# Row gathers regrouped into bursts of 8, 12 and 12, and a part of the second layer moved, in a DLRM interaction tower

## What is computed

```python
e = stack([tbl_f[ids[:, f]] for f in range(27)], axis=1)      # 2048 x 27 x 128
dot = einsum('bnd,bmd->bnm', e, e)                             # 2048 x 27 x 27
z = the 351 entries of dot with n < m
h = concatenate([z, dense_ctx], axis=1)                        # 2048 x 367
h = maximum(h @ W_top1 + b_top1, 0)                            # 367 x 512
h = maximum(h @ W_top2 + b_top2, 0)                            # 512 x 256
y = h @ W_top3                                                 # 256 x 1
```

## Time and profile before

| | us |
|---|---|
| median of 3 executions | 512.14 (509.94 to 519.04) |
| profiled execution, own time | 503.7 |
| its span | 501.9 |
| mean granted TensorE clock | 0.864 of full speed |

### The profile page before, as it was taken

How to read it: one execution, slowest core, us unless ns; L and a number is a source line. 1 busy time by engine, 2 the same in 40 slices (tenths; PEclk the granted TensorE clock), 3 DMA queues, 4 the chain that set the end, 5 groups by cost and what they waited for, 6 DMA issues and landing times.

```text
span 501.9 us, 14882 instructions
## 1 busy us (share of the span) xinstructions
PE 377.5 (75%) x6214; PEld 340.0 (68%) x6214; DVE 234.1 (47%) x505; ACT 130.5 (26%) x165; POOL 286.9 (57%) x264
## 2 busy tenths in 40 slices
PE   2578466289569977699919995699786988299997
PEld 2477356189458966499707984689675987289786
DVE  4766081257215663166612872165631636338241
ACT  2265010124012232033301340122320313123432
POOL 5888667763455744465663845467544767638300
PEclk9959579579788997799957997799967999789999
DMA  7995312212112131133122131132211231111100
GB/s 193 271 253 147 120 46 74 53 34 96 34 44 76 47 106 31 31 86 110 32 52 63 44 106 37 37 76 56 96 36 28 74 120 32 49 26 35 28 1 0
DMA packets 22270, 36.18 MB, mean 72 GB/s; under 512 B 12662, under 2 KB 13310, under 8 KB 22252
## 3 DMA queue, kind: packets, MB, share of 16 engines
q1 hardware_dynamic: 13996, 19.01, 13.2%
q0 software_dynamic: 8256, 16.92, 12.8%
HBM read 35.90 MB, written 0.01 MB: 72 GB/s over the span
## 4 chain that ended last, share of the span: by engine, by line
PE 66%; issue 21%; another core or an unknown queue 4%; DMA 3%; DVE 2%; ACT 2%; SPq 1%; ACTq 0%; DVEq 0%
PE emb_ps L693 30%; PE gram_ps L738 13%; PE mlp_ps L761 7%; PE emb_ps L729 5%; PE mlp_ps L775 3%; PE emb_ps L709 3%; DMA ids_b<-in_ids_mm 3%; PE mlp_ps L783 2%; DVE onehot L564 2%; PE emb_ps L828 1%; PE mlp_ps L745 1%; ACT embT L459 1%; SPq L276 1%; PE emb_ps L840 1%
## 5 line engine op out<-in xcount | busy, mean ns | idle before, releaser
L415 POOL DMA_INDIRECT rows<-in_tbl,idx x256 | 279.9, 1093 | 181.4 <-PE gram_ps L738 53.3
L693 PE MATMUL emb_ps<-onehot,parts 125*128 125x256 f32 x1280 | 171.8, 294 | 34.5 <-issue 15.1
L693 PEld LDWEIGHTS emb_ps<-onehot,parts 125*128 125x128 f32 x1280 | 163.7, 198 | 42.9 <-issue 22.3
L564 DVE TENSOR_SCALAR onehot<-ids_b,row_of 128x512 fp32r<-128x512 int32 x320 | 131.1, 483 | 85.7 <-PE emb_ps L693 46.8
L738 PE MATMUL gram_ps<-embT 128*32 128x26 f32 x4096 | 72.3, 217 | 79.0 <-issue 78.9
L738 PEld LDWEIGHTS gram_ps<-embT 128*32 128x32 f32 x4096 | 61.4, 136 | 93.3 <-issue 93.1
L451 ACT ACTIVATE embT<-emb_ps 128x512 f32<-128x512 f32 x40 | 49.0, 1224 | 141.4 <-PE emb_ps L693 91.6
L586 DVE STREAM_TRANSPOSE turned<-gram_ps 128x832 f32<-128x832 f32 x16 | 16.8, 1050 | 128.9 <-PE gram_ps L738 121.1
L459 ACT ACTIVATE embT<-emb_ps 128x512 f32<-128x512 f32 x32 | 36.8, 1241 | 81.2 <-PE emb_ps L729 62.8
L580 DVE COPY embT<-emb_ps 128x512 f32<-128x512 f32 x32 | 36.1, 1184 | 22.0 <-PE emb_ps L729 9.7
L729 PE MATMUL emb_ps<-ident,rows 128*128 128x128 f32 x256 | 36.2, 296 | 4.2 <-issue 3.1
(11 more groups left out here) (40 smaller groups left out, 105.7 us busy)
## 6 DMA issues: line engine op xcount, KB each, us to landing
ids_b<-in_ids_mm SPq DMA_DIRECT2D x8, 896.0 KB
ids_b<-in_ids_mm SPq DMA_DIRECT2D x16, 256.0 KB
rows<-in_tbl,idx POOLq DMA_INDIRECT x256
embT<-in_tbl SPq DMA_DIRECT2D x6, 448.0 KB
w_sb<-in_tbl SPq DMA_DIRECT2D x2, 448.0 KB
turned<-in_tbl SPq DMA_DIRECT2D x1, 560.0 KB
w_sb<-in_W_top SPq DMA_DIRECT2D x1, 512.0 KB
turned<-in_tbl SPq DMA_DIRECT2D x1, 448.0 KB
```

The lines of the kernel that those rows point to most:

```text
L415: pool.indirect_dma_start(rows[:, t, n, :], None, tables[f], bass.IndirectOffsetOnAxis(idx[:, t, f:f + 1], 0), engine_sem=gathers_written) ...
L564: last = nc.vector.tensor_scalar(onehot[:, k % OH:k % OH + LOOK_TABLES, c, :], ids_b[:, k:k + LOOK_TABLES, :], row_of[:, c:c + 1], None, A ...
L693: last = nc.tensor.matmul(emb_ps[BANK[k]][:, m * W:(m + 1) * W], parts[0:MP, f, part, c * D:(c + 1) * D], onehot[0:MP, f % OH, c, :], star ...
```

## The change

POOL's waits are regrouped. Counted again from the pair before, no gather follows the transposes of tile 0; eight (groups 0 and 1 of tile 0) follow Gram 0, twelve (groups 2 and 3 of tile 0, group 0 of tile 1) follow Gram 1, and twelve (groups 1 to 3 of tile 1) follow lookup 4 of the pair itself. A wait of POOL at the end of pair 0 goes, which the first group of pair 1 now has itself. On TensorE four of the eight calls of the second layer go ahead of the transposes of tile 1.

```diff
-CALLS_AFTER = [{3: 6}, {3: 8}]
+CALLS_AT = [{NT: 6}, {0: 4, NT: 4}]
...
                 if isinstance(p, int) and p == 0:
                     return
-                if t == 0:
-                    if k == 1:
-                        pool.wait_ge(emb_filled, (p - 1) * JOBS + row_job(0, NT - 1) + 1)
-                    elif k == 2:
-                        pool.wait_ge(gram_filled, (p - 1) * TILES + 1)
-                    elif k == 3:
-                        pool.wait_ge(emb_filled, (p - 1) * JOBS + row_job(1, NT - 1) + 1)
-                elif k == 0:
-                    pool.wait_ge(gram_filled, p * TILES)
+                if t == 0 and k % 2 == 0:
+                    pool.wait_ge(gram_filled, (p - 1) * TILES + 1 + k // 2)
+                elif t and k == 1:
+                    pool.wait_ge(emb_filled, p * JOBS + 4)
                 else:
-
-                    pool.wait_ge(emb_filled, p * JOBS + k)
+                    return
                 pool.sem_inc(pool_waited, 1)
...
-                if first:
-
-                    pool.wait_ge(gram_filled, 1)
-                    pool.sem_inc(pool_waited, 1)
...
                 for t in range(TILES):
                     calls = 0
-                    for k in range(NT):
-                        transpose_rows(p, t, k)
-                        for _ in range(0 if first else CALLS_AFTER[t].get(k, 0)):
+                    for k in range(NT + 1):
+                        for _ in range(0 if first else CALLS_AT[t].get(k, 0)):
                             (first_layer_rest, second_layer)[t](p - 1, calls)
                             calls += 1
+                        if k < NT:
+                            transpose_rows(p, t, k)
                     gram(p, t)
```

## The result

| | before | after |
|---|---|---|
| median of 4 executions, us | 511.04 (506.94 to 519.04) | 568.07 (563.42 to 571.22) |
| profiled execution, own time / span, us | 503.7 / 501.9 | 571.22 / 569.4 |
| mean granted TensorE clock | 0.864 | 0.823 |

The ratio is 1.114, 95% interval 1.102 to 1.126: slower by 57 us. The forecast was 506.0 us in a range of 489 to 531, so it was wrong, and the nearest of the rivals is the first (near 560). The profiled execution of before is one of its fastest (503.7 against a median of 511.04), so the two spans differ by more than the medians, 67.5 us.

A forecast was written before the change was run, and what follows sets the result against it. TensorE held 66% of the chain of waits, and a Gram under gathers was taken to stall until they end. Pair 1 -7.0, five steady pairs -5.0, pair 7 +5.9: -6.1, so 506 us, range 489 to 531.

The forecast's parts named there:

- The burst of twelve behind Gram 1: Twelve gathers under lookups 1 to 3; lookups bear it, nothing taken, range 0 to 2 us a pair.
- The window of 16.4 us: Twelve gathers from 158.9 to 175.3 in the kernel before, with TensorE busy throughout; taken as showing that lookups bear gathers.
- The first rival: Burst behind Gram 1 stalls the lookups as in pair 1: about 9.5 us in six pairs, near 560; chance 0.22.
- The pause of 2 us: Behind Gram 1, between four gathers and twelve more in the kernel before; its loss was priced at nothing.
- The rest of the steady pair: Gram 0 ends at 42.7 instead of 43.4, Gram 1 gains nothing; 1.0 us less a pair, -5.0 for five.
- Its trickle ending 1.2 us behind a gather: Gram 0 of pairs 2 to 6 stays in two pieces, its slow part ending 1.2 us behind the last gather.
- The half second layer: Four calls ahead of tile 1's transposes, 1 to 2 us, hidden by Gram 1's trickle; worth nothing.
- Pair 1: Shorter gather run, TensorE back near 95.9 instead of 102.1: 6.2 us, with Gram 0's 0.7 us taken as -7.0.
- the second burst's part: Twelve gathers behind lookup 4: Gram 0 meets their tail and ends 0.7 us earlier, also counted in pair 1.
- Pair 7: Gram 0, free of gathers before, now meets the burst behind lookup 4 and ends at 484.3 instead of 478.4: +5.9 us.
- Second rival: One-hots block a gather, Gram 0 slips through early: 2.1 to 3.5 us less in six pairs, 490 to 498; chance 0.20.
- Third rival: Pair 1's stall doesn't form: pair 1 takes 58 instead of 76 us, -18 instead of -7, 495 total; chance 0.13.

The follow-up runs named there:

- e15: Changed kernel with a 128 x 256 scratch fill on POOL ahead of only the twelve gathers behind Gram 1: 509.24 us, ratio 1.012.
- e10: Changed kernel with POOL filling a 128 x 256 scratch tile ahead of each gather: 489.94 us, ratio 0.962.
- e14: Changed kernel with a small 128 x 8 scratch fill on POOL ahead of each gather: 573.75 us, ratio 1.136.
- e17: Changed kernel with a 128 x 128 scratch fill on POOL ahead of each gather: 556.70 us, ratio 1.089.
- e1: Changed kernel with the burst of twelve behind Gram 1 paused after four gathers, until lookup 1 is done: 512.13 us, ratio 1.015.
- e4: Changed kernel with eleven extra one-hot operations a pair on VectorE, written to a tile nobody reads: 523.31 us, ratio 1.038.
- e5: Changed kernel with the burst behind Gram 1 paused after eight gathers, until lookup 2 is done: 547.51 us, ratio 1.066.
- e3: Kernel before with only the second layer's four calls moved ahead of tile 1's transposes: 508.27 us, ratio 1.011.
- e16: Changed kernel with the 128 x 256 fill ahead of each gather and without the wait for lookup 4: 482.81 us, ratio 0.946.
- e2: Kernel before without POOL's three waits for lookups 1 to 3, so sixteen gathers follow Gram 1 in one run: 597.62 us, ratio 1.185.

## Why the prediction was wrong

**The step that failed** is "The burst of twelve behind Gram 1 ... By the 16.4 us window the lookups bear it; I take nothing, with 0 to 2 us a pair as the range". It costs 10 us a pair in pairs 2 to 6: lookup 3 ends at +24.1 in place of +14.1, and with this burst alone spaced (e15) the loss goes from 11.4 to 1.2%. The window of 16.4 us was right and was read for the wrong thing. There VectorE made one-hots, so its gathers lay 1.41 us apart on average ((174.39 - 158.93) / 11); behind Gram 1 VectorE is idle and they lie 1.25 apart. I had both figures in the same paragraph (16.4 us "under one-hots", "at the pitch without them" 15.0 us) and used them for the burst's length only, not as a difference in kind. Which of the two spacings is safe is what e10, e14 and e17 show.

**The first rival** named the pattern, the place and the price: 9.5 us a pair against 10.4 measured. On top of the forecast that gave 555 us in the profiled execution and 563 in the median, against 571.2 and 568.1. What it lacked is mostly in pair 7, where its stall met the later Gram 0. It got 0.22. What I held against it, that the burst begins behind a finished Gram and not under one, was not evidence: no row of before showed a long run of close gathers under lookups that was harmless. The only such run, in pair 1, had stalled. With that said the rival should have been the forecast.

**The pause of 2 us** stood in the prediction ("There stood four, a pause of 2 us, and twelve more"), and I priced its loss at nothing. e1 shows that it is worth ten per cent of the time. As e1, e4 and e5 read together, it lets lookup 1's signal out, VectorE starts, and from then on VectorE's work keeps the gathers apart. That order of causes is my reading; a pause that waits for no signal wasn't tried, and in pairs 1 and 7 of the changed kernel the signal came in time and lookup 3 was late even so. e5 shows that its place matters.

**The rest of the steady pair**, judged by e1, where lookups are whole: predicted 57.4 on average, measured 59.3 (57.4 to 62.9). Gram 0 was to end at +42.7 and ends at +42.6 in pair 2, which is luck, by two errors that cancel: the burst ended at +36.8 instead of +38.8, since its gathers lay 1.31 us apart and not 1.41, and Gram 0 came 5.8 us behind it instead of 3.9, in one piece and not in two. "Its trickle ending 1.2 us behind a gather" is wrong there: the signals of tile 0's transposes are late under a close burst, and Gram 0 doesn't start until it is over (188.08 in e1, with the last gather issued until 185.55). So it is in pairs 2, 3 and 6 of e1 and in pairs 2 to 5 of the changed kernel; in pairs 4 and 5 of e1 Gram 0 came in pieces and ended at +42.2. The half second layer, taken as hidden, costs at most 1.2 us a pair and perhaps nothing (e3).

**Pair 1**, predicted -7.0: with the start it gave -1.4 in the changed kernel and -2.5 in e1. The recovery that I foresaw at 95.9 came at 96.96, 5.2 us sooner than in before. But Gram 0 of pair 1 then waited for the signals under the burst behind lookup 4: it ended at 134.33, against 135.92 in before. What failed here is the second burst's part, which I had as a gain of 0.7 us. **Pair 7**, predicted +5.9: +17.0, with the stall of the lookups in it (lookup 3 ends at +21.9 in place of +14.0). In e1 it is +7.9 and in e10 +6.4, which is the term about as I worked it out.

**Second rival** (one-hots block a gather, Gram 0 slips through): in pairs 2 to 6 of the changed kernel no gather lasted over 1.3 us, so it didn't occur. The rule of the Trainium skill that it drew on (page "SBUF — State Buffer", section "Who interferes with whom") has no part in the result that a row shows. **Third rival** (pair 1's stall doesn't form): it formed, though shorter; start and pair 1 together took 149.8 us.

## What stays open

What inside the chip is held up isn't shown. It isn't transfer capacity (17 to 21% busy in the trickle), nor the limit on queued gathers (the same in e10 as in the changed kernel), nor the second layer. It isn't the loading of code either: between 153 and 501 us the changed kernel's trace has no packet of the instruction queues, and the stalls of pairs 2 to 6 lie in that stretch. TensorE stops between records of one row, and signals that others wait for come out late, both while the run of gathers lasts; in pair 2 until its end, in pairs 3 and 4 some microseconds before it. Whether one causes the other, or both come from a third thing, no run here could tell. Why e16 stalls in pair 4 and hardly in the others is open as well. Each execution here has its span and clock from the profiler's records and none was timed without them, so that the recording has a part in it isn't excluded.

## What to carry to other kernels

A run of row gathers issued back to back by POOL can stop TensorE and hold back the signals for VectorE and ScalarE, as here, so look at the spacing of the gathers, start to start, and not only at how long they take or how busy the DMA is; here 1.25 and 1.34 us stalled, and 1.45 us didn't but for one pair of e16. A wait that looks like a loss (two idle microseconds on an engine off the critical path) may be what breaks such a run: before taking it out, find a place in the same trace where the work goes on without it, with the same engines busy and idle. A stall that shows once in a trace, in pair 1, is a warning about each place that the change makes like it.

## What the hardware showed that I had not expected

- Work of no use on POOL, 0.33 to 0.50 us ahead of each gather, took the changed kernel from a ratio of 1.114 to one of 0.962, and before to 0.979.
- The lateness of signals reaches 10 us: lookup 1 filled its bank at 155.1, and two engines saw it at 165.0. In pair 2 of e2 it is 12.0 us (167.16 to 179.17).
- POOL's fills and VectorE's one-hots slow each other down, without either being shut out. The first row is e10's one-hots, the second its fills; in the changed kernel the same one-hots took 481 ns on average, and a fill that runs alone takes 0.33 us.

```profile
L559 DVE TENSOR_SCALAR onehot<-ids_b,row_of 128x512 fp32r<-128x512 int32 x320 | 170.9, 606 | 47.0 <-PE emb_ps L688 32.8
...
L385 POOL MEMSET extra<- 128x256 f32 x258 | 103.3, 400 | 54.1 <-PE gram_ps L733 40.1
```

- The Trainium skill, page "SBUF — State Buffer", section "SBUF: two separate sides", says in substance that TensorE has ports of its own and never waits on another engine or on DMA there. The trace neither bears that out nor refutes it: TensorE does wait under close gathers, for up to 1.7 us between two matmuls, and the profile doesn't name the path.
- The granted clock was 0.79 and 0.83 over pairs 1 and 2 of the changed kernel; in the 9.7 us around the trickle it was 0.75, full until 160.9 and at the lower level (0.50) from there. TensorE made 6 records in the 3.2 us at full clock and 5 in the 4.8 us behind them, and was busy for 4.30 of the 9.70 us, so it waits at either level and the clock is a small part of the loss.
